# A two-layer selective-scan network on one core: softplus as one ScalarE function, four states a pass weighed by GpSimd, images without a loop

## What is computed

```python
x_dbl = einsum('bkdl,kcd->bkcl', xs, x_proj_weight)       # 12 + 16 + 16 rows: dt, B, C
delta = softplus(dt_proj(dts) + dt_projs_bias)
h = exp(delta * A) * h + (delta * u) * B                  # 16 states for each channel
y = sum over states of h * C, plus D * u
```

```python
dt = softplus(dt @ W_dt + b_dt)
decay = exp(cumsum(dt * A))
h = decay * cumsum(dt * B * u / (decay + 1e-12))
y = sum over states of h * C, plus D * u
```

## Time and profile before

| | |
|---|---|
| median of three runs | 17376.94 us (17374.18 to 17382.03) |
| the profiled execution, its span | 17392.46 us, 17390.7 us |
| mean granted clock of TensorE | 0.912 |
| busy share | DVE 89%, POOL 84%, PE 75%, ACT 55% |
| one image: start of layer 0 to its first scan | 2176 to 2266 us |
| scans of layer 0 with the tail's beginning | 2266 to 3612 us |
| passage to layer 1 | 3612 to 3721 us |
| scans of layer 1 and tail | 3721 to 4350 us |

### The profile page before, as it was taken

One profiled execution on the slowest core, in us unless ns is written; L12 is line 12 of the kernel. 1 busy time (PEld: TensorE's weight loads), 2 busy tenths in 40 slices (PEclk: granted clock), 3 DMA queues, 4 the chain that ended last, 5 costly groups with the idle time before them and its releaser, 6 DMA issues.

```text
span 17390.7 us, 131294 instructions
## 1 busy us (share of the span) xinstructions
PE 13112.4 (75%) x29696; PEld 5217.6 (30%) x29696; DVE 15474.8 (89%) x9374; ACT 9648.6 (55%) x9235; POOL 14596.9 (84%) x6213
## 2 busy tenths in 40 slices
PE   6777777777777777777777777777777777777777
PEld 2322323223232232322323223232232322323223
DVE  8998889988899888998889988899888998889988
ACT  4555745557455574555745557455564555645556
POOL 8996779967799677996789967899678996789967
PEclk9998989989899898998989989899898998989989
DMA  4552245522455224552245522455224552245522
GB/s 159 183 178 81 74 158 183 178 81 74 158 182 179 81 75 158 184 179 81 73 160 182 179 81 73 161 182 180 80 73 159 183 180 80 74 161 183 178 79 74
DMA packets 662535, 2348.09 MB, mean 135 GB/s; under 512 B 75452, under 2 KB 97224, under 8 KB 661704
## 3 DMA queue, kind: packets, MB, share of 16 engines
q1 hardware_dynamic: 661704, 2339.01, 39.2%
HBM read 2322.98 MB, written 15.73 MB: 134 GB/s over the span
## 4 chain that ended last, share of the span: by engine, by line
POOL 38%; PE 22%; issue 17%; DVE 10%; DMA 9%; ACT 3%; POOLq 1%; DVEq 0%; SPq 0%; ACTq 0%
POOL room L834 26%; PE bank L474 12%; DMA room<-bc_rows 9%; DVE room L1092 5%; POOL room L843 4%; PE bank L354 4%; PE bank L483 3%; POOL room L792 2%; DVE room L1112 2%; POOL room L817 2%; PE bank L508 2%; POOL room L811 2%; DVE room L1075 1%; DVE room L1013 1%; ACT room L706 1%
## 5 line engine op out<-in xcount | busy, mean ns | idle before, releaser
L834 POOL TENSOR_TENSOR room<-room 128x1024 f32<-128x1024 f32 x3072 | 7180.8, 2366 | 15.3 <-DVE room L1013 7.3
L1013 DVE TENSOR_TENSOR_SCAN room<-bank,room 128x1024 f32<-128x1024 f32 x3072 | 6971.9, 2281 | 163.5 <-issue 75.5
L426 PE MATMUL bank<-room,identity 128*128 128x512 f32 x12288 | 6193.3, 631 | 177.3 <-DVE y L1032 162.5
L613 ACT ACTIVATE bank<-room,a 128x1024 f32<-128x1024 f32 x3072 | 3420.6, 1116 | 4182.6 <-DVE room L1013 4178.2
L474 PE MATMUL bank<-room,identity 128*128 128x512 f32 x6144 | 3136.9, 658 | 1229.4 <-DVE room L1112 908.5
L1092 DVE TENSOR_TENSOR_SCAN room<-bank,room 128x1024 f32<-128x1024 f32 x1536 | 3440.2, 2275 | 19.9 <-POOL room L889 4.0
L1021 DVE TENSOR_TENSOR room<-room,bank 128x1024 f32<-128x1024 f32 x2544 | 3049.7, 1199 | 392.9 <-PE bank L413 390.9
L426 PEld LDWEIGHTS bank<-room,identity 128*128 128x128 f32 x12288 | 2391.6, 198 | 2660.0 <-issue 2064.5
L413 PE MATMUL bank<-parts,pick_row 96*128 96x512 bf16 x5088 | 1587.8, 394 | 1918.7 <-DVE room L1021 1846.8
L889 POOL TENSOR_TENSOR room<-room 128x1024 f32<-128x1024 f32 x768 | 2326.2, 3052 | 60.9 <-POOL room L881 60.9
L474 PEld LDWEIGHTS bank<-room,identity 128*128 128x128 f32 x6144 | 1257.6, 210 | 3047.2 <-issue 2676.3
(11 more groups left out here) (97 smaller groups left out, 11555.4 us busy)
## 6 DMA issues: line engine op xcount, KB each, us to landing
room<-bc_rows SPq DMA_DIRECT2D x4368, 512.0 KB, 4.2
wx<-in_w_x SPq DMA_DIRECT2D x65, 162.0 KB
bc_rows<-xdbl SPq DMA_DIRECT2D x72, 128.0 KB, 4.3
xT<-in_x SPq DMA_DIRECT2D x8, 768.0 KB, 5.5
out_x<-xT SPq DMA_DIRECT2D x8, 768.0 KB, 4.4
win<-in_w_in SPq DMA_DIRECT2D x16, 288.0 KB, 3.3
room<-in_w_in SPq DMA_DIRECT2D x16, 288.0 KB, 4.0
room<-in_w_out SPq DMA_DIRECT2D x16, 288.0 KB, 4.3
```

What stands on the lines that cost most here:

```text
L426: ins = nc.tensor.matmul(bank[:, YACC + h, :], identity[:, :], state0[:, g % STATES, halves(h)], start=(n == 0), stop=(n == N - 1))
L613: nc.scalar.activation(whole(DECAY0[g % 2]), delta0[:, j, :], ACT.Exp, scale=a0[:, col:col + 1]).then_inc(S["decay"], note("decay", (i, j, ...
L834: nc.gpsimd.tensor_tensor(source0[:, g % SOURCES, :], du0[:, j, :], b_ring0[:, g % BROWS, :], ALU.mult).then_inc(S["source"], note("source ...
L1013: nc.vector.tensor_tensor_scan(run(state0[:, g % STATES, :]), run(whole(DECAY0[g % 2])), run(source0[:, g % SOURCES, :]), 0.0, ALU.mult, A ...
```

## The change

- ACT's Softplus function takes the place of the steps on three engines. In layer 0 a whole dt (both halves) is projected by PE in one piece at n = 5, copied by ACT at unit n = 6 behind its decay, and turned into delta at n = 2 of the next pass, for the pass after that one. In layer 1 Softplus reads PSUM.
- POOL weighs n = 2, 5, 8, 11 in every pass but those with j = 2, where it is 5, 8, 11 (all four in the last order): 89 units of 384 instead of 66. The x projections move from j = 1 to j = 0, n = 8 and 11, and the gate's pieces and SP's load of the x weights move too.
- du is made at n = 6. The second du of an image is no longer made ahead of the first source.
- The running sums of layer 1 are made in the order 2, 0, 1, 3, so that one in row order is first.
- The repeated norm goes from (7, 0, 9) to (6, 2, 9).
- The loop over images is written out, so semaphore targets are constants.

```diff
+SUMS1 = (2, 0, 1, 3)
 def by_pool(i, j, n):
-    return n in (8, 11) or n in (2, 5) and (j == 1 or i == K - 1 and j > 0)
+    return n in ((5, 8, 11) if j == 2 and i < K - 1 else (2, 5, 8, 11))
...
 def piece(g):
     ahead = i * J + j + 2
-    if n in (8, 11):
-        if ahead < PASSES:
-            return "dt", ahead // J, ahead % J, int(n == 11)
-        if (i, j) == (K - 1, 1):
-            return "z", 0, 1, int(n == 11)
-    if n in (2, 5):
-        if j == 1 and i < K - 1:
-            return "xd", i + 1, int(n == 5)
-        if i == K - 1 and j > 0:
-            return "z", 0, 0 if j == 1 else 2, int(n == 5)
+    if n == 5 and ahead < PASSES:
+        return "dt", ahead // J, ahead % J
+    if j == 0 and n in (8, 11) and i < K - 1:
+        return "xd", i + 1, int(n == 11)
+    if i == K - 1:
+        return {(0, 2): ("z", 0, 0, 0), (0, 8): ("z", 0, 0, 1), (0, 11): ("z", 0, 1, 0),
+                (1, 2): ("z", 0, 1, 1), (1, 8): ("z", 0, 2, 0), (1, 11): ("z", 0, 2, 1)}.get((j, n))
...
 SyncE, rows0:
-                    if (j, n) == (1, 1) and i + 2 < K:
-                        sp.wait_ge(S["mm"], at("mm", ("dt", 0, i, J - 1, 1), b))
+                    if (j, n) == (0, 8) and i + 2 < K:
+                        sp.wait_ge(S["mm"], at("mm", ("dt", 0, i, J - 1), b))
                         load_wx(i + 2)
...
 TensorE:
-            def dt_proj(b, l, i, j, h):
+            def dt_proj(b, l, i, j, banks=WORK):
                 w = wdt[XR:XR + R, i % 2, :] if l == 0 else wdt1[XR:XR + R, :]
-                work(b, h, ("dt", l, i, j, h), [("ev", ("xd", l, i, h))],
-                     [(w[:, j * P:(j + 1) * P], xdbl[XR:XR + R, halves(h)])])
+                if banks == WORK:
+                    wait_free(b, 0, 1)
+                    free[0] = free[1] = ("ev", ("dt", l, i, j))
+                for h in range(2):
+                    pe.wait_ge(S["ev"], at("ev", ("xd", l, i, h), b))
+                    ins = nc.tensor.matmul(bank[:, banks[h], :], w[:, j * P:(j + 1) * P], xdbl[XR:XR + R, halves(h)],
+                                           start=True, stop=True)
+                ins.then_inc(S["mm"], note("mm", ("dt", l, i, j)))
 (layer 0 begins with j=0 in WORK and j=1 in SPARE, layer 1 with j=0, 1, 2 in WORK, YACC and HSUM)
...
 ScalarE (take_dt of Abs and Relu, exponent, plus_one, logarithm, minus_one go):
+            def take_dt(b, i, j, lo=WORK[0]):
+                act.wait_ge(S["mm"], at("mm", ("dt", 0, i, j), b))
+                nc.scalar.activation(delta0[:, j, :], whole(lo), ACT.Copy).then_inc(
+                    S["ev"], note("ev", ("dt", 0, i, j)))
+            def softplus(b, i, j):
+                act.wait_ge(S["ev"], at("ev", ("dt", 0, i, j), b))
+                nc.scalar.activation(delta0[:, j, :], delta0[:, j, :], ACT.Softplus,
+                                     bias=dtb0[:, SCANS[i][0], j:j + 1]).then_inc(S["dl"], note("dl", (0, i, j)))
+            def softplus1(b, j, lo):
+                act.wait_ge(S["mm"], at("mm", ("dt", 1, 0, j), b))
+                nc.scalar.activation(delta1[:, j, :], whole(lo), ACT.Softplus,
+                                     bias=dtb1[:, j:j + 1]).then_inc(S["dl"], note("dl", (1, 0, j)))
...
 ScalarE, scans0, start, then the loop over g behind decay(b, g) and the xd or z piece of g - 2:
+                take_dt(b, 0, 0)
+                softplus(b, 0, 0)
+                take_dt(b, 0, 1, SPARE[0])
+                second_part(b, 0, 0)
+                second_part(b, 0, 1)
...
+                    p = piece(g - 1)
+                    if p and p[0] == "dt":
+                        take_dt(b, p[1], p[2])
+                    ahead = i * J + j + 1
+                    if g < len(UNITS) and n == 2 and ahead < PASSES:
+                        softplus(b, ahead // J, ahead % J)
                     if g < len(UNITS) and j == 2 and n in (6, 7) and i + 1 < K:
                         second_part(b, i + 1, n - 6)
...
 ScalarE, scans1:
+                softplus1(b, 0, WORK[0])
                 columns(0)
+                softplus1(b, 1, YACC)
+                softplus1(b, 2, HSUM)
...
 GpSimd, scans0 (correction, add_log, correct go):
                 du(b, 0, 0, 0)
-                du(b, 0, 0, 1)
...
-                        if n == 9:
-                            du(b, 0, ahead // J, ahead % J)
+                    if n == 6 and ahead < PASSES:
+                        du(b, 0, ahead // J, ahead % J)
...
 VectorE (correction, add_log, correct go in both layers):
-                    if (i, j, n) == (K - 1, 0, 9):
+                    if (i, j, n) == (K - 2, 2, 9):
                         norm_again(b, 0)
...
-                for q in range(Q):
+                for q in SUMS1:
                     sum_of_steps(0, q)
...
-                        sum_of_steps(j + 1, n // 2 - 2)
+                        sum_of_steps(j + 1, SUMS1[n // 2 - 2])
...
 all engines (here TensorE; build(counts, images) passes 1 and then NB):
-            with pe.Fori(0, NB) as b:
+            for b in range(images):
```

More of the change, by code:

```diff
@@ L206, in program @@
         rows_open = semaphore("rows_open")
-        def wait_delta(engine, b, i, j):
-            kind = "dl" if i * J + j < 2 else "dl_pool"
-            engine.wait_ge(S[kind], at(kind, (0, i, j), b))
         def halves(h):
@@ L323, in image @@
                 sp.wait_ge(S["res"], at("res", (1, 1), b))
-                dst = out[slice(b, b + 1) if isinstance(b, int) else bass.ds(b, 1), :, :]
+                dst = out[b:b + 1, :, :]
                 sp.dma_start(dst.rearrange("o (h p) t -> p (o h) t", p=CH), xT[:, :, :]).then_inc(store_done, 16)
@@ L329, in _ @@
             load_win(0, win0_loaded)
-            before = dict(counts.now)
-            if NB > 1:
-                with sp.Fori(0, NB - 1) as b:
-                    image(b, True)
+            for b in range(images):
+                image(b, b + 1 < images)
+                if b + 1 < images:
                     load_x(b + 1)
-            counts.now = before
-            image(NB - 1, False)
         @block.tensor
@@ L432, in scans0 @@
                     x_proj(b, 0, 0, h)
-                for j in range(2):
-                    for h in range(2):
-                        dt_proj(b, 0, 0, j, h)
+                dt_proj(b, 0, 0, 0)
+                dt_proj(b, 0, 0, 1, SPARE)
                 for g in range(len(UNITS) + 1):
@@ L457, in scans1 @@
                     x_proj(b, 1, 0, h)
-                for j in range(J):
-                    for h in range(2):
-                        dt_proj(b, 1, 0, j, h)
+                for j, banks in enumerate((WORK, (YACC, YACC + 1), (HSUM, HSUM + 1))):
+                    dt_proj(b, 1, 0, j, banks)
                 def add_direction(m, q):
@@ L577, in second_part @@
                     S["p2"], note("p2", (0, i, c)))
-            def delta_of(l, j):
-                return delta0[:, j, :] if l == 0 else delta1[:, j, :]
-            def take_dt(b, l, i, j, h):
-                bias = dtb0[:, SCANS[i][0], j:j + 1] if l == 0 else dtb1[:, j:j + 1]
-                take(b, ("dt", l, i, j, h), soft[l][j][:, halves(h)], h, func=ACT.Abs, bias=bias)
-                nc.scalar.activation(delta_of(l, j)[:, halves(h)], bank[:, WORK[h], :], ACT.Relu, bias=bias).then_inc(
-                    S["ev"], note("ev", ("dt", l, i, j, h)))
@@ L668, in scans1 @@
                 take_xd(b, 1, 0, 1)
-                for j in range(J):
-                    for h in range(2):
-                        take_dt(b, 1, 0, j, h)
-                for j in range(J):
-                    exponent(b, 1, 0, j)
-                    plus_one(b, 1, 0, j)
-                    logarithm(b, 1, 0, j)
                 def columns(j):
@@ L772, in _ @@
             act.wait_ge(setup, 6)
-            with act.Fori(0, NB) as b:
+            for b in range(images):
                 front(b, 0)
@@ L901, in _ @@
             make_taps(0)
-            with pool.Fori(0, NB) as b:
+            for b in range(images):
                 scans0(b)
@@ L1035, in scans0 @@
                 init_y(b, 0)
-                for j in range(2):
-                    correction(b, 0, 0, j)
-                    add_log(b, 0, 0, j)
-                    correct(b, 0, 0, j)
-                    if j == 0:
-                        third_part(b, 0)
+                third_part(b, 0)
                 for g in range(len(UNITS) + 1):
@@ L1057, in scans1 @@
                 init_y(b, 1)
-                for j in range(J):
-                    correction(b, 1, 0, j)
-                    add_log(b, 1, 0, j)
-                    correct(b, 1, 0, j)
                 def sum_of_steps(j, q):
-                    if q == 0 and j >= 2:
+                    if q == SUMS1[0] and j >= 2:
                         dve.wait_ge(S["gate"], at("gate", (j - 2, N - 1, Q - 1), b))
@@ L1170, in _ @@
             dve.wait_ge(setup, 6)
-            with dve.Fori(0, NB) as b:
+            for b in range(images):
                 front(b, 0)
```

(6 more changed lines are left out.)

98 lines of the change are left out of this document (10 added, 88 removed).

## The result

| | before | after |
|---|---|---|
| time, us | 17379.49 (17374.18 to 17382.15, 4 runs) | 17105.31 (17099.35 to 17106.73, 4 runs) |
| profiled execution, us (span) | 17392.46 (17390.7) | 17104.75 (17103.0) |
| granted clock of PE, mean | 0.912 | 0.912 |
| instructions | 131294 | 102091 |

The change makes the kernel 274 us faster: ratio 0.9843, 95% interval 0.983 to 0.9855. The forecast was 17090, range 16860 to 17290.

The account below looks back on a forecast made before the run. POOL bound layer 0's scans by a little, DVE after the change; the starts were chains. Per image 16.8 + 22.6 - 6.7 (scans) + 3 (images written out) = 35.7 us, 286 over eight: 17090 us, range 16860 to 17290.

Parts of the forecast that it names:

- (a): Scans of layer 0: POOL loses 66 softplus steps and gains 23 weighings; DVE loses 25.5 us an image and binds.
- Rival B: POOL still binds in the scans of layer 0 despite its lighter load: 17280 us, chance 0.07.
- (e): ACT's softplus and table loads in layer-0 scans: 5.9 us before a decay wanted at 8.9, so hidden.
- (f): SP's load of B row 9 in layer 0 waits for the dt; its source is still ready in time, so hidden.
- (b): DVE's idle time in layer-0 scans: 32 us for x projections stay, the other 33 fall to 12 an image.
- (c): ACT's dt copy ahead of decay(7) stalls DVE 2.1 us at scan(7): 46.2 us an image, plus 7.0 in j=2.
- rival C: PE's granted clock falls in the scans of layer 0, making the kernel slower: 17641 us, chance 0.06.
- (d): PE's spread of unit 6, behind the dt copy and sum(4), arrives before weigh(6) can start: no cost.
- The starts: First scan of layer 0 comes 16.8 us earlier, first scan of layer 1 22.6 us earlier, per image.
- Rival A: No dt stall, as something else is late at n=6 anyhow: 16665 us, chance 0.14.

Follow-up runs that it names:

- Experiment 7: 5 plus idle PE matmuls at n = 2, with POOL weighing n = 5, 8, 9, 11, 12 in passes j = 0 of orders 3 to 6; 16896.87 us.
- 11: The changed kernel with two more ACT copies of delta ahead of each softplus in the scans of layer 0; 17124.93 us.
- experiment 3: The changed kernel with POOL weighing only n = 5, 8, 11 in every pass of the first seven orders; 17121.11 us.
- experiment 1: The changed kernel with ACT's copy of a dt one unit later, behind decay(7) instead of ahead of it; 16860.75 us.
- 5: experiment 1 plus PE's sum of the unit before a piece placed behind the next spread instead of ahead of it; 16849.01 us.
- experiment 2: The kernel before the change with only its loop over images written out; 17371.94 us.
- 10: The changed kernel with the running sums of layer 1 back in the order 0, 1, 2, 3; 17129.28 us in one run.
- 9: The changed kernel with the edits of experiment 1 and experiment 3 together, the sums left where they were; 16853.53 us.
- 8: 5 with the edit of experiment 3, so POOL doesn't weigh n = 2 in the first seven orders; 16743.14 us.

## Why the prediction was right, step by step

- **Bound.** DVE binds after (a), and POOL never does: no scan of layer 0 waits for it, where 8.1 us did. Rival B falls. Experiment 7 shows how near it is.
- **(a), (e), (f)** stand, (f) by its end only: the row of B for unit 9 comes 2 to 7 us too late for POOL in five passes of an image, 26 us in all, where POOL hardly waited for a row before. But no scan waits for POOL, so it is hidden. For (e) see 11.
- **(b)** kept 44.5 us of idle time, 32 for the x projections and 12 for the rest. Measured beside ACT's 69.2 are 34.9, nearly all for PE's spread. The x projections are as forecast (idle time at their spreads 32.8); of the rest some 2 us are left for 12.
- **(c)** named the right wait at the right unit. Its size, 2.1 us for one dt, is right where PE runs at full clock (1.95). The mean isn't: 69.2 us an image where 46.2 and 7.0 make 53.2. The term that is mis-sized is "I take 2.1": its upper bound, 3.8 by a dt at 1.2 GHz, is what several passes show, up to 4.87 where the sum ahead is slow too. The 16 us between them are the hole at n = 2: in experiment 3, without it, the wait is 52.6. The prediction had such holes, and the dt at half clock, as rival C and as a bound, and put them at nothing in its sum.
- **(d)** holds for the changed kernel, where the weighing of unit 6 waits 1.5 us an image. It was worked out with every sum and dt at full clock, and the spread is in truth free only because DVE stands still for decay(7): without that stall half of it comes back as a wait for the spread (1 and 5).
- **The norm** wasn't in the sum. Its two steps together take half as long at their new place. Before, then after (the third number is a mean: 9.4 and 0.8 us before, 2.1 and 2.8 after):

```profile
L999 DVE TENSOR_SCALAR room<-xT,gs,rstd 96x1024 f32<-96x1024 f32 x2 | 10.2, 5122 | 0.0
```

```profile
L914 DVE TENSOR_SCALAR room<-xT,gs,rstd 96x1024 f32<-96x1024 f32 x2 | 4.9, 2486 | 0.0
```

  5.3 us an image for the better. So the +6.1 of the stage meets the forecast of +6.7 by errors that cancel: +16.0 for the dt, -9.6 for the other idle time, -5.3 for the norm. They make +1.1 where the stage has -0.6; the 1.7 between them is about what the scans of layer 0 lost in experiment 2, by the images written out alone. That the stage's number came out so near is luck in this sense; the range would have held without it.
- **The starts**, 16.8 and 22.6, came at 16.5 and 23.9. In the start of layer 0 the chain is as worked out up to the decay, but DVE's third part, 2.94 us instead of about 1.3, ends it. In the passage the bound is POOL's chain (10), as forecast: 3698.5 there was POOL's end, not DVE's. These 40 us an image, more than the whole gain, are read from the chains in the traces; no run has the new softplus alone.
- **Rival A** (no dt stall) is refuted by 551.5 us of it, and experiment 1 gives its price, 245 us. **Rival C**: the stage's clock is 0.92 for 0.94, not 0.90; its mechanism is there, in the passes with a hole at n = 2 (the 16 us of (c)), at a size that the other terms hide.

## What to carry to other kernels

When a piece is moved in an in-order queue, work out not only who waits behind it but which queue inherits the wait when it is taken away: here a copy one unit later took 551 us of waits and gave 249 back at the next engine. Cost a fourth unit handed to a less busy engine with the holes it leaves in the engine that used to serve it: 14 weighings an image, 124 us of VectorE's time, were worth 16 at most in the changed kernel, which is within the noise, and cost 106 in the better one. Edits that each gain nothing may gain together (5 and 9 against 8); as their traces read, either alone left one item too many in the same gap. The version with all three, 16743 us, beats both kernels, 0.9634 of the time before.

## What the runs showed of the hardware

- The same four matmul records of a dt took 1.95 us in one pass and 3.78 in the next order, with PE's 3.1 us of idleness at n = 2 and a spread at 1.01 for 0.59 ahead of the slow ones. A sum fell from 1.88 to 3.64 us behind a dt at full clock and no pause, too (9). A higher mean clock isn't a faster kernel: 0.934 in 9 at 16854 us, 0.923 in 8 at 16743, 0.912 in the changed kernel.
- Softplus from SBUF takes 1.15 us for 1024 columns, from PSUM 1.11, and a table load 1.28, with nothing visible around it.
- A VectorE step with a scalar column (96 partitions, 1024 columns, L999) took 9.4 us while GpSimd made products one behind the other, and the same step right behind it 0.80. At another place of the pass the two took 2.1 and 2.8. Alone, ahead of the scans, the same shape takes 0.81 (a group of 32 in the whole run: 806 ns). What sets how long such a step is held up is not shown.
- A VectorE product of 32 partitions with both inputs in SBUF (the third part) took 1.22 us where it began 0.05 us ahead of a GpSimd product, and 2.94 where it began 0.5 us behind one.
